# Moving the last FFN normalisation from GpSimd to VectorE in a fused attention and FFN block

## What is computed

```python
x = x + attn(layernorm(x), W_qk, W_v, slope)      # causal, with a distance bias
x = x + ffn(layernorm(x), w_gate, w_up, w_down)   # hidden width 384, int weights / 127

gate = einsum('bsd,hd->bsh', x, wg)
up   = einsum('bsd,hd->bsh', x, wu)
h    = silu(gate) * up
out  = einsum('bsh,dh->bsd', h, wd)
```

## Time and profile before

| | us |
|---|---|
| median of 3 runs | 142.77 |
| lowest, highest | 142.57, 145.8 |
| the profiled execution | 142.62 |
| its span | 140.60 |

### The profile page before, as it was taken

One profiled execution on the slowest core, in us unless ns is written; L12 is line 12 of the kernel. 1 busy time (PEld: TensorE's weight loads), 2 busy tenths in 40 slices (PEclk: granted clock), 3 DMA queues, 4 the chain that ended last, 5 costly groups with the idle time before them and its releaser, 6 DMA issues.

```text
span 140.6 us, 3402 instructions
## 1 busy us (share of the span) xinstructions
PE 119.5 (85%) x1183; PEld 87.7 (62%) x1183; DVE 118.9 (85%) x336; ACT 109.2 (78%) x249; POOL 103.3 (73%) x162
## 2 busy tenths in 40 slices
PE   0249658999999999989999998997998579999970
PEld 0047245867988778977869975766742436666750
DVE  0739989998696999899987969998869999999891
ACT  4034688999976999957999949977959779999820
POOL 6391779973994354997795999469757999999800
PEclk9999999999999999999999999999999999999998
DMA  4897000000000000000000001443000312738407
GB/s 129 242 231 198 1 2 2 5 2 0 5 0 0 5 0 2 0 5 0 0 5 0 0 5 37 93 98 79 0 5 0 79 37 42 75 78 242 137 12 216
DMA packets 18515, 7.28 MB, mean 52 GB/s; under 512 B 9152, under 2 KB 18496, under 8 KB 18496
## 3 DMA queue, kind: packets, MB, share of 16 engines
q1 hardware_dynamic: 18496, 7.02, 20.7%
HBM read 2.82 MB, written 2.10 MB: 35 GB/s over the span
## 4 chain that ended last, share of the span: by engine, by line
PE 42%; DVE 31%; ACT 15%; issue 4%; DMA 3%; SPq 2%; DVEq 1%
DVE probsT_lo L833 5%; PE work_ps L557 5%; DVE hidden_lo L957 4%; PE attn_ps L570 4%; PE attn_ps L571 3%; PE attn_ps L572 3%; ACT probs L996 3%; DVE biased L850 3%; PE score_ps L591 3%; DMA wd_int<-in_L_ffn_w_down_dram 3%; PE score_ps L505 3%; PE score_ps L594 3%; DVE hidden L870 3%; PE score_ps L507 3%; PE score_ps L506 3%
## 5 line engine op out<-in xcount | busy, mean ns | idle before, releaser
L833 DVE TENSOR_TENSOR probsT_lo<-work_ps,probsT_hi 128x512 f16<-128x512 f32 (+3 forms) x48 | 25.1, 552 | 3.8 <-ACT probsT_hi L1018 3.5
L570 PE MATMUL attn_ps<-v_hi,probsT_hi 128*128 128x128 f16 x144 | 25.8, 219 | 2.4 <-DVE xs L860 1.7
L996 ACT ACTIVATE probs<-biased,neg_max 128x128 f32<-128x128 f32 (+7 forms) x32 | 25.1, 783 | 3.2 <-DVE neg_max L850 3.1
L850 DVE CUSTOM_DVE_ANT_0 biased<-score_ps,bias,neg_score_scale 128x128 f32<-128x128 f32 (+7 forms) x32 | 25.7, 803 | 0.6 <-PE score_ps L507 0.6
L1018 ACT CAST probsT_hi<-work_ps 128x512 f16<-128x512 f32 (+3 forms) x48 | 21.4, 484 | 5.7 <-PE work_ps L557 5.4
L572 PE MATMUL attn_ps<-v_hi,probsT_lo 128*128 128x128 f16 x144 | 25.8, 219 | 0.0
L571 PE MATMUL attn_ps<-v_lo,probsT_hi 128*128 128x128 f16 x144 | 25.7, 219 | 0.0
L557 PE MATMUL work_ps<-ident,probs 128*128 128x128 f32 x144 | 21.4, 274 | 0.7 <-DVE probsT_lo L833 0.7
L557 PEld LDWEIGHTS work_ps<-ident,probs 128*128 128x128 f32 x144 | 16.5, 141 | 3.7 <-DVE probsT_lo L833 1.0
L735 DVE BATCH_NORM_STATS2 stats<-xs 128x6 f32<-128x128 f32 x64 | 15.2, 280 | 3.7 <-DMA xs<-in_L_attn_x_dram 3.7
L570 PEld LDWEIGHTS attn_ps<-v_hi,probsT_hi 128*128 128x128 f16 x144 | 14.1, 98 | 5.5 <-DVE probsT_lo L833 1.8
(11 more groups left out here) (138 smaller groups left out, 331.1 us busy)
## 6 DMA issues: line engine op xcount, KB each, us to landing
out_dram<-xs SPq DMA_DIRECT2D x7, 256.0 KB, 2.8
xs<-in_L_attn_x_dram SPq DMA_DIRECT2D x3, 512.0 KB, 7.9
xs<-in_L_attn_x_dram SPq DMA_DIRECT2D x2, 256.0 KB, 3.1
out_dram<-xs SPq DMA_DIRECT2D x2, 128.0 KB, 2.5
wgu_int<-in_L_ffn_w_gate_dram SPq DMA_DIRECT2D x1, 192.0 KB, 2.9
wgu_int<-in_L_ffn_w_up_dram SPq DMA_DIRECT2D x1, 192.0 KB, 3.0
wd_int<-in_L_ffn_w_down_dram SPq DMA_DIRECT2D x1, 192.0 KB, 4.5
x2T_hi<-xn_hi SPq DMA_TRANSPOSE x8, 2.5
```

Source lines behind the costliest of these rows:

```text
L570: pe.matmul(attn_ps[:, 0:D], p_hi, v_j, start=(j == 0), stop=False)
L833: dve.tensor_tensor(probsT_lo[:, i % 2, cols], work_ps[:, bank, 0:n], probsT_hi[:, i % 2, cols], ALU.subtract).then_inc(work_emptied, 1)
L850: dve.tensor_tensor_reduce(biased[:, i % 2, 0:n], score_ps[:, i % 2, 0:n], bias[:, S - n:S], neg_score_scale[:, 0:1], 3.0e38, ALU.add, ALU ...
L996: act.activation(probs[:, i % 2, 0:n], biased[:, i % 2, 0:n], ACT.Exp, bias=neg_max[:, i:i + 1], scale=-1.0, accum_out=prob_sum[:, i:i + 1 ...
```

## The change

Four things are done together.

1. **Round 7 is normalised on VectorE.** GpSimd's `centre(B + 3)` and `scale(B + 3)` go, four 128x512 operations. A new `normalise_last` does it with eight 128x128 `tensor_scalar` operations, four for each half. The first half stands ahead of blocks 0 and 1 of `multiply(2)`, the second between these and block 2. ScalarE's `token_high` of that round waits for a new semaphore.
2. **GpSimd takes more low parts.** By chunk, 0 to 7, its blocks go from 0, 1, 2, 2, 2, 2, 2, 1 to 0, 3, 2, 2, 3, 3, 2, 1, in sum from 12 to 16; VectorE's from 12 to 8. None of chunk 1 is left to VectorE.
3. **The tokens of round 6 are cast earlier.** Both `token_high(B + 2, h)` move from behind `silus(1)` and `silus(2)` to between blocks 1 and 2 of `silus(0)`, and those of round 7 come one chunk earlier.
4. **GpSimd's order.** `token_low(B + 2, 0)` comes ahead of `moments(B + 3)`, `token_low(B + 2, 1)` right behind it and ahead of `hidden_low(1)`.

```diff
         def pool_blocks(c):
-            return 0 if c == 0 else 1 if c in (1, NCH - 1) else HB - 1
+            return (0, 3, 2, 2, 3, 3, 2, 1)[c]
...
             norm(B + 2)
+            token_low(B + 2, 0)
             moments(B + 3)
-            token_low(B + 2, 0)
-            centre(B + 3)
+            token_low(B + 2, 1)
             hidden_low(1)
-            scale(B + 3)
-            token_low(B + 2, 1)
+            token_low(B + 3, 0)
             hidden_low(2)
-            token_low(B + 3, 0)
             hidden_low(3)
             token_low(B + 3, 1)
...
+            def normalise_last(h):
+                n = B + 3
+                if h == 0:
+                    dve.wait_ge(pool_step, steps_before(n) + N_SMALL)
+                    dve.wait_ge(xn_lo_ready, split_before(n - 1, 0))
+                for j in range(CT * h, CT * h + CT):
+                    m = dve.tensor_scalar(xn[:, n % 2, j, :], xs[:, NT - TB + j, :], mean[:, 1, j:j + 1], rstd[:, 1, j:j + 1],
+                                          ALU.subtract, ALU.mult)
+                m.then_inc(last_xn_ready, 1)
...
             for j in range(HB):
                 multiply(1, [j])
                 hidden_low(0, [j])
-            hidden_low(1)
-            for c in range(LAG, NCH - 1):
+            normalise_last(0)
+            multiply(LAG, range(HB - 1))
+            normalise_last(1)
+            multiply(LAG, range(HB - 1, HB))
+            add_ffn(0)
+            hidden_low(LAG)
+            for c in range(LAG + 1, NCH - 1):
...
-                act.wait_ge(xn_ready, HALVES * n + h)
+                if n == B + 3:
+                    act.wait_ge(last_xn_ready, h + 1)
+                else:
+                    act.wait_ge(xn_ready, HALVES * n + h)
...
-            silus(0, 0)
+            silus(0, 0, range(EARLY))
+            for h in range(HALVES):
+                token_high(B + 2, h)
+            silus(0, 0, range(EARLY, HB))
...
-                for n, h in {1: [(B + 2, 0)], 2: [(B + 2, 1)], 3: [(B + 3, 0)], 4: [(B + 3, 1)]}.get(c, []):
+                for n, h in {2: [(B + 3, 0)], 3: [(B + 3, 1)]}.get(c, []):
```

## The result

| | before | changed |
|---|---|---|
| lowest, highest execution, us | 142.57, 145.85 | 145.28, 147.29 |
| median of 6 executions, us | 144.28 | 146.79 |
| profiled execution, us | 142.62 | 146.85 |
| its span, us | 140.60 | 145.1 |

The ratio is 1.0264, with a 95% interval of 1.0173 to 1.0356: slower, though the interval doesn't say whether by 2%. The forecast was 146.8 us, in a range of 142.1 to 148.2.

What follows compares the result with a forecast made beforehand. It took TensorE's stretch from 113.30 to 134.80 us, without slack, as the bound, so a late start costs in full. 3.7 us at block 2 of `gate_up(3)` plus 0.5 after it, on 142.6, gave 146.8 us, range 142.1 to 148.2.

Steps and rivals of the forecast that it cites:

- The mechanism: On VectorE, each `tensor_scalar` of `normalise_last` draws SBUF in two streams and waits for a whole GpSimd instruction, 1.2 us each.
- The pattern of which of the eight wait: On VectorE, first two `tensor_scalar` wait, third and fourth don't; fifth waits to 115.1, sixth to 116.3, seventh to 117.5.
- the price of one meeting: On VectorE, a `tensor_scalar` that waits for one GpSimd instruction costs 1.12 + 0.1 = 1.2 us.
- The step `hidden_low(0, [1])`: On VectorE, this low part, due at 107.09, meets GpSimd's `token_low` and ends at 108.6 instead of 107.7.
- The +0.5 for what follows: After block 2 of `gate_up(3)`: low-part waits in chunks 3 and 6 and the end, together -0.4 to +1.5, taken as +0.5.
- less 0.4 at the end: At the last `multiply` on VectorE, no low-part wait ahead of it: last results up to 0.4 us sooner.
- The sum: Whole kernel: 3.7 + 0.5 = 4.2 us added to the profiled 142.62 us, giving 146.8 us.
- the forecast's 3.7: On TensorE, block 2 of `gate_up(3)` starts at 118.7 instead of 115.04, 3.7 us lost, including 0.7 at its start.
- Casts moved forward at no cost: Round 6's casts and first `token_low` fit idle gaps of ScalarE and GpSimd, delaying `moments` by 0.1 us; no gain either.
- The first, that the operations don't wait: On VectorE, the `tensor_scalar` take 0.26 us each without waiting: 142.1 to 143.3, say 142.5 us; chance 0.26.
- The second, that only the first of four waits: On VectorE, only the first `tensor_scalar` of each four waits for GpSimd: say 144.4 us; chance for only some waiting 0.13.
- The third: TensorE's gap ahead of `gate_up(3)` closes wholly, gaining 2.3 us plus 0.4 at the end: 139.9 us; chance 0.04.

Runs made afterwards that it cites:

- the last version: Changed kernel with all eight `tensor_scalar` behind `add_ffn(0)`, round 7's casts later, `token_low(B + 2, 1)` behind `hidden_low(1)`, other low-part shares: 141.28 us, ratio to before 0.9917.

## Why the prediction came out, point by point

**The mechanism** was right, shown by the waits themselves and by the two kernels in which they vanish (with the accumulator; with GpSimd idle). The pattern of which of the eight wait is the forecast's, down to the fifth, which waited only for the rest of a `token_low` (0.73 us in all, forecast 0.6).

**Its size.** The forecast put block 2 of `gate_up(3)` at 118.7, 3.7 us late; measured 118.26, 3.2 us. The term that was too large is the price of one meeting. I took 1.12 + 0.1 = 1.2 us; it is 1.11, as GpSimd isn't held up by the short operation: its low parts there last 1.15 us, against 1.60 beside a low part of VectorE. The step `hidden_low(0, [1])` ending at 108.6 measured 108.72; `down(0)` forecast from 110.3, measured 110.42; `gate_up(3)` forecast at 114.0, measured 113.90.

**The +0.5 for what follows** was right for a wrong reason. It was to be made of low parts of chunks 3 and 6 that meet GpSimd, up to 0.8 each, less 0.4 at the end. Both low parts lasted 0.71 us: VectorE didn't wait. They did meet GpSimd, but it was GpSimd that paid (its instruction behind each, at 122.81 and 135.16, lasts 1.60 us instead of 1.15), off the path. The end did give 0.4: VectorE's last operations start 4.48 us later than before, where TensorE's stretch was 4.87 later. What took the place of the other term is the clock at 1.2 GHz, 1.65 us, which the forecast didn't have at all. The trace of before showed no lower clock behind an idle time of 2.1 us; but the forecast took its 145.8 us for mere spread, and it made two such gaps with only 1.7 us of work between them and didn't ask what that does to the clock.

**The sum.** Forecast 3.7 + 0.5 = 4.2. Measured 3.22 + 1.65 - 0.39 = 4.48, and the spans differ by 4.5. Two errors, -0.5 and +0.8, mostly cancel, and that the median came out at 146.79 for 146.8 is luck. In the two executions at the higher clock the time is 145.3, where the forecast's 3.7 alone, without its +0.5, gave 146.3, and with the 0.4 gained at the end 145.9.

**Casts moved forward at no cost.** Right as to TensorE's start: alone they left `gate_up(3)` where it was, and they bring nothing by themselves. (`token_low` ahead of `moments` put it off by 0.2 us, not 0.1.) Who pays where a low part meets GpSimd's earlier work is decided within hundredths of a microsecond: in the changed kernel the starts are 0.04 us apart (107.09 and 107.13) and VectorE waits, with the casts alone 0.03 us and GpSimd waits, though its row starts first in both.

**The rivals.** The first, that the operations don't wait, is what the accumulator form imitates, and its sum came out near: block 2 of `gate_up(3)` at 115.4 (its forecast 114.4, with operations of 0.26 instead of 0.33 us), 141.95 us against 142.5 in a range from 142.1. The second, that only the first of four waits, is excluded by the rows. The third is partly real: in the last version the gap ahead of `gate_up(3)` is closed, one of 1.05 us is left ahead of `gate_up(4)`, and it reaches 141.3 us, short of 2% gain.

## What to carry to other kernels

Before work is moved from GpSimd to VectorE, ask whether it reads SBUF in two streams, and what GpSimd will run beside it: eight short operations cost 2.1 us in a silent stretch and 4.6 to 6.0 us in a busy one. Many small operations are a bad shape for this, as each may wait for a whole GpSimd instruction (that fewer and larger ones do better was not run). A form that reads a single stream can be the faster one though it is slower by itself, 0.40 for 0.34 us; but the one tried here writes other values than the normalised ones, so it serves only where those can be used. And don't put them between two operations for which TensorE waits: a gap there costs itself, and in some executions a stretch at half the clock. So look at the clock of every execution before two kernels are compared.

## What the runs showed of the hardware

- A 128x128 `tensor_scalar` between SBUF tiles, with two column operands, takes 0.34 us, or 1.19 us behind a 128x512 GpSimd subtract. GpSimd pays nothing for it (1.15 us), though it pays 0.45 us for a two-input subtract of VectorE.
- With an accumulator output the same operation takes 0.40 us, and none of eight waited beside GpSimd.
- GpSimd's power on 128x8 (1.63 us) doesn't hold up VectorE's two-input subtract: of the changed kernel, the one at 105.87 lies wholly within it:

```profile
105.87 0.68 DVE L966 TENSOR_TENSOR hidden_lo<-hidden,hidden_hi 128x512 f16<-128x512 f32 x1
105.50 1.64 POOL L361 TENSOR_TENSOR rstd<-var_eps,norm_const 128x8 f32<-128x8 f32 x1
```

- In the changed kernel TensorE's clock fell to 1.2 GHz at about 119 us, when it was at work again, after idle times of 1.2, 2.0 and 2.5 us; it was back to 2.4 GHz before 123 us. It also fell behind a single idle time of 2.13 us (casts and token parts alone, 114.0 to about 117.4 us), and it didn't behind the same one in before's trace, nor behind idle times of 1.2, 1.5 and 2.5 us with the old shares. It varies from execution to execution.
